# Four expert layers: router product turned round, low part of the router weights made later, sparse expert weights kept in fp32

## The reference

```python
x = x + _L0_ffn_ref(_layernorm(x), w12, w3, router_w, expert_bias, sw1, sw2, sw3)   # f1, f2
x = x + _L1_ffn_ref(_layernorm(x), gate_w, wg, wu, wd)                              # f3, f4

# f1, f2: a shared part of width 1024, and 8 routed experts of width 128, two for each token
shared_out = silu(x @ sw1.T) * (x @ sw2.T) @ sw3.T
scores = sigmoid(x @ router_w.T)                      # [1024, 8]
_, top_idx = top_k(scores + expert_bias, 2)
# f3, f4: 16 routed experts of width 128, two for each token, no shared part
scores = softmax(x @ gate_w.T)                        # [1024, 16]
topk_w, topk_idx = top_k(scores, 2)                   # then divided by their sum
# both: for each chosen expert e of token t, with weight c
y_t += c * (silu(x_t @ wg_e) * (x_t @ wu_e)) @ wd_e
```

## Time and profile before

| | us |
|---|---|
| median of three runs | 1898.88 (1898.35 to 1899.68) |
| the profiled execution | 1904.39 |
| its span | 1902.6 |
| PE busy in it | 1559.5 (82%) |
| DVE busy | 1293.0 (68%) |
| ACT busy | 931.7 (49%) |
| POOL busy | 680.3 (36%) |

### The profile page before, as it was taken

The page is one execution under the profiler, slowest core; times in us unless marked ns, Lnnn a source line. Parts: engine busy times, 40 slices in busy tenths (PEclk is TensorE's granted clock), DMA queues, the critical chain, the costliest instruction groups (busy, mean ns, idle before and its releaser), DMA issues. The chain is left out here.

```text
span 1902.6 us, 28081 instructions
## 1 busy us (share of the span) xinstructions
PE 1559.5 (82%) x9276; PEld 1211.8 (64%) x9286; DVE 1293.0 (68%) x2184; ACT 931.7 (49%) x2281; POOL 680.3 (36%) x711
## 2 busy tenths in 40 slices
PE   6899799879974665491679999999999999999472
PEld 5444478667851222480668888888888888887372
DVE  4665374666466998754647777777777777776652
ACT  2365345233524331451556666666666666665351
POOL 3011243315366773445823333222222233330173
PEclk9899799888986888595889999999999999999586
DMA  3220323223310000564000000000000000000463
GB/s 79 51 50 3 96 88 110 70 72 106 106 51 1 0 1 14 163 145 131 11 0 12 12 12 1 23 1 23 1 23 1 23 1 12 1 1 1 139 147 109
DMA packets 62057, 90.01 MB, mean 47 GB/s; under 512 B 10192, under 2 KB 44240, under 8 KB 61920
## 3 DMA queue, kind: packets, MB, share of 16 engines
q1 hardware_dynamic: 53664, 65.68, 11.6%
q0 software_dynamic: 8256, 22.56, 5.3%
HBM read 62.38 MB, written 19.40 MB: 43 GB/s over the span
## 5 line engine op out<-in xcount | busy, mean ns | idle before, releaser
L1295 DVE TENSOR_REDUCE gqa_neg_max<-acc 128x1 f32<-128x1024 f32 (+7 forms) x256 | 193.0, 754 | 173.8 <-PE acc L1404 172.7
L1181 ACT ACTIVATE gqa_probsT_high<-aux 128x512 fp32r<-128x512 f32 x288 | 172.0, 597 | 249.5 <-PE aux L1412 248.7
L1300 DVE TENSOR_TENSOR gqa_probsT_low<-aux,gqa_probsT_high 128x512 fp32r<-128x512 f32 x288 | 197.6, 686 | 29.8 <-ACT gqa_probsT_high L1181 25.6
L1190 ACT ACTIVATE gqa_probs<-acc,gqa_neg_max 128x1024 f32<-128x1024 f32 (+7 forms) x256 | 189.3, 740 | 29.7 <-DVE gqa_neg_max L1295 24.7
L1412 PE MATMUL aux<-ident,gqa_probs 128*128 128x128 f32 x1152 | 174.3, 274 | 0.0
L1088 POOL TENSOR_SCALAR gqa_q_scale<-gqa_q_scale 128x4 f32<-128x4 f32 x64 | 16.3, 255 | 382.1 <-ACT gqa_square L1125 381.8
L474 POOL DMA_INDIRECT f_xs<-tokens,f_slot_token x108 | 116.6, 1080 | 100.3 <-DVE f_slot_token L631 48.9
L1423 PE MATMUL aux<-gqa_probsT_high,gqa_v_high 128*128 128x512 f32 x288 | 146.5, 509 | 1.0 <-DVE gqa_probsT_low L1300 1.0
L1435 PE MATMUL aux<-gqa_wo,gqa_oT 128*128 128x256 f32 x512 | 133.3, 383 | 4.4 <-DVE stream L1288 3.5
L1092 POOL TENSOR_TENSOR gqa_ln_xn<-gqa_ln_xn 128x512 f32<-128x512 f32 x64 | 82.3, 1285 | 146.3 <-DVE gqa_ln_xn L1220 146.3
L1402 PE MATMUL acc<-gqa_k_low,gqa_q_high 128*128 128x512 f32 (+5 forms) x384 | 132.2, 344 | 0.0
(11 more groups left out here) (411 smaller groups left out, 4397.5 us busy)
## 6 DMA issues: line engine op xcount, KB each, us to landing
f_w<-in_f_up SPq DMA_DIRECT2D x64, 256.0 KB, 3.6
outputs_by_slot<-f_y_tile SPq DMA_DIRECT2D x108, 128.0 KB, 2.3
f_w<-in_f_down SPq DMA_DIRECT2D x64, 128.0 KB, 3.8
mat_qk<-mat_high SPq DMA_DIRECT2D x64, 64.0 KB, 2.3
tokens<-f_ln_xn SPq DMA_DIRECT2D x4, 1024.0 KB, 4.4
gqa_w_q<-in_g_wq SPq DMA_DIRECT2D x8, 512.0 KB, 3.5
gqa_wo<-in_g_wo SPq DMA_DIRECT2D x8, 512.0 KB, 3.8
mat_qk<-mat_low SPq DMA_DIRECT2D x32, 64.0 KB, 2.3
```

Source lines behind the costliest of these rows:

```text
L1181: act.activation(probsT_high[:, u % RING, :], aux[:, u % 2, :], ACT.Copy).then_inc(cell_high_ready, 1)
L1190: act.activation(out, scores(n), ACT.Exp, bias=neg_max[:, j % (2 * JOBS):j % (2 * JOBS) + 1], accum_out=row_sum[:, n // 2 % 4, m, n % 2:n ...
L1295: dve.tensor_reduce(neg_max[:, j % (2 * JOBS):j % (2 * JOBS) + 1], scores(n), AXY, ALU.max, negate=True).then_inc(max_ready, 1)
L1300: dve.tensor_tensor(probsT_low[:, u % RING, :], aux[:, u % 2, :], probsT_high[:, u % RING, :].bitcast(F32), ALU.subtract).then_inc(cell_lo ...
```

## The change

- The router's product is turned round. High and low parts of the router weights stand side by side in one tile, `w_router_parts`. They stand still, and 256 tokens run past them: `route_high` for the tokens' high part gives the products with both weight parts on 16 or 32 partitions, and `route_low` adds the tokens' low part times the high weights. They are issued between the transposes of the norm. ACT copies each result to `logits_by_expert` (which lies in `xs`, not yet in use), and `by_token` brings it back to a token on each partition, in fp32, with a matrix `sum_parts` that adds the two parts.
- The low part of the router weights and `sum_parts` are made within the norm on DVE, ahead of the first low part of the tokens.
- The routed experts' weights are loaded straight into `ws` in fp32. They are not split. One copy `part` in fp32 takes the place of `part_high` and `part_low`, and each product of three fp32r matmuls becomes one fp32 matmul. SP no longer waits for room in the ring for these experts. The ring and the splits stay for the shared experts.
- The copy to `y_tile` moves from ACT to DVE, behind `s_hidden`. In f3 and f4 Exp stands ahead of the splits' old place, with one Silu of one column behind it.

```diff
+            if q == 3 and before_low:
+                before_low()
             if q >= 3:
                 low(q - 3)
...
-            for m, e in enumerate(LOADS):
-                if m == STAGES:
+            for i, e in enumerate(LOADS):
+                if i == STAGES:
                     sp.wait_ge(norm.xn_ready, NT)
                     sp.dma_start(tokens_dram.rearrange("(n p) d -> p n d", p=P), norm.xn[:, :, :]).then_inc(xn_stored, 16)
+                if e not in place:
+                    sp.dma_start(ws[:, e - shared, 0:UP], up_dram[e:e + 1].rearrange("a p k n -> (a p) (k n)")).then_inc(ws_in, 16)
...
+                    continue
...
-                    act.activation(part_high[:, n % 3, cols], aux[:, n % 2, cols], ACT.Copy).then_inc(part_high_ready, 1)
+                    act.activation((part if PLAIN else part_high)[:, n % 3, cols], aux[:, n % 2, cols], ACT.Copy).then_inc(part_high_ready, 1)
...
-            dve.wait_ge(w_router_high_ready, 1)
-            dve.tensor_tensor(w_router_low[:, :, :], w_router[:, :, :], w_router_high[:, :, :].bitcast(F32),
-                              ALU.subtract).then_inc(w_router_low_ready, 1)
-            norm.vector(dve)
-            split(0)
...
+            norm.vector(dve, router_parts)
+            if shared:
+                split(0)
...
             else:
-                for m in range(1, E // 2):
-                    split(m)
                 dve.wait_ge(logits_ready, 1)
...
+                    if n >= 4 and PLAIN:
+                        m = n - 4
+                        dve.wait_ge(risen, n)
+                        if m >= 4:
+                            dve.wait_ge(y_stored[m % 4], 16 * (m // 4))
+                        dve.tensor_copy(y_tile[:, m % 4, :], aux[:, 2 + n % 2, D:2 * D]).then_inc(y_ready, 1)
...
-            for t in range(NT):
-                pe.wait_ge(norm.low_ready, t // 2 + 1)
...
-                    for m, (a, b) in enumerate(three(core.xnT_high[:, k, rows], core.xnT_low[:, k, rows],
-                                                     w_router_high[:, k, :], w_router_low[:, k, :])):
...
+            def route_high(q):
...
+                for k in range(DC):
+                    pe.matmul(route_banks[q][0:PAIR, 0:2 * P], w_router_parts[:, k, :],
+                              core.xnT_high[:, k, tokens], start=k == 0, stop=False, skip_group_check=True)
...
+            norm.tensor(pe, route)
+            route_low(2)
+            route_high(3)
+            by_token(0)
+            route_low(3)
+            for q in range(1, 4):
+                last = by_token(q)
             last.then_inc(logits_ready, 1)
```

More of the change, by code:

```diff
@@ L208, in tensor, with scalar @@
             last.then_inc(self.turned, 1)
-    def scalar(self, act):
+            if after:
+                after(q)
+    def scalar(self, act, after=None):
         c = self.core
@@ L232, in ffn_layer @@
     FRONT = 8
+    PAIR = 2 * routed
     LOADS = (0, 8, 9, 1, 10, 11, 2, 12, 13, 3, 14, 15, 4, 5, 6, 7) if shared else tuple(range(E))
-    place = {e: m for m, e in enumerate(LOADS)}
-    by_pool = [shared > 0 and e >= shared for e in LOADS]
+    PLAIN = True
+    RINGED = [e for e in LOADS if not (PLAIN and e >= shared)]
+    by_pool = [shared > 0 and e >= shared for e in RINGED]
+    place = {e: m for m, e in enumerate(RINGED)}
     splits = {2: (4, 5, 6), 3: (7, 8), 4: (9, 10), 5: (11,), 6: (12,), 7: (13,)}
@@ L246, in dense @@
         def dense(i):
-            steps.extend(("split", m) for m in splits.get(i, ()))
+            steps.extend(("split", place[LOADS[m]]) for m in splits.get(i, ()) if LOADS[m] in place)
             steps.extend([("up", i), ("silu", i)])
@@ L271, in sparse @@
             if shared and s in (2, 4):
-                steps.append(("split", 13 + s // 2))
+                steps.append(("split", place[LOADS[13 + s // 2]]))
             if s >= 1:
@@ L403, in w_split @@
         def w_split(m):
-            e = LOADS[m]
+            e = RINGED[m]
             if e >= shared:
@@ L460, in _ @@
                       allow_small_or_imprecise_dtypes=True).then_inc(numbers_made, 1)
-            for m in range(E):
+            for m in range(len(RINGED)):
                 if by_pool[m]:
@@ L510, in _ @@
             else:
-                for m in range(1, E):
-                    split(m)
+                act.wait_ge(shifted, 1)
+                act.activation(probs[:, :, :], select[:, :, :], ACT.Exp).then_inc(exp_ready, 1)
+                act.activation(s_silu[:, 0, 0:1], core.minus_half[:, 0:1], ACT.Silu)
             for kind, n in steps:
@@ L596, in _ @@
                 hide(0)
-                split(3)
+                split(place[1])
                 hide(1)
@@ L672, in _ @@
                                       ALU.subtract).then_inc(low_ready, 1)
-                elif kind == "part":
+                elif kind == "part" and not PLAIN:
                     cols = part_cols(n)
@@ L785, in rise @@
                         rows = slice(k * P, (k + 1) * P)
-                        for m, (a, b) in enumerate(three(part_high[:, r, rows], part_low[:, r, rows],
-                                                         *sparse_weights(s - 1, slice(k * 2 * P, (k + 1) * 2 * P)))):
-                            last = pe.matmul(aux[:, 2 + s % 2, 0:D], a, b, start=k + m == 0, stop=(k, m) == (DC - 1, 2))
+                        pairs = sparse_pairs(r, rows, s - 1, slice(k * 2 * P, (k + 1) * 2 * P))
+                        for m, (a, b) in enumerate(pairs):
+                            last = pe.matmul(aux[:, 2 + s % 2, 0:D], a, b, start=k + m == 0, stop=(k, m) == (DC - 1, len(pairs) - 1))
@@ L789, in rise @@
                 if s >= 4:
-                    for m, (a, b) in enumerate(three(part_high[:, r, D:], part_low[:, r, D:],
-                                                     *sparse_weights(s - 4, slice(UP, UP + D)))):
-                        last = pe.matmul(aux[:, 2 + s % 2, D:2 * D], a, b, start=m == 0, stop=m == 2)
+                    pairs = sparse_pairs(r, slice(D, D + P), s - 4, slice(UP, UP + D))
+                    for m, (a, b) in enumerate(pairs):
+                        last = pe.matmul(aux[:, 2 + s % 2, D:2 * D], a, b, start=m == 0, stop=m == len(pairs) - 1)
@@ new lines, in route_low, with by_token @@
+            def route_low(q):
+                tokens = slice(2 * q * P, (2 * q + 2) * P)
+                pe.wait_ge(norm.low_ready, q + 1)
+                for k in range(DC):
+                    last = pe.matmul(route_banks[q][0:routed, 0:2 * P], w_router_parts[:, k, 0:routed],
+                                     core.xnT_low[:, k, tokens], start=False, stop=k == DC - 1, skip_group_check=True)
+                last.then_inc(routed_ready, 1)
+            def by_token(q):
+                pe.wait_ge(parts_copied, q + 1)
+                for t in (2 * q, 2 * q + 1):
+                    last = pe.matmul(aux[:, 2, t * routed:(t + 1) * routed], logits_by_expert[:, t * P:(t + 1) * P],
+                                     sum_parts[:, :], start=True, stop=True, skip_group_check=True)
+                return last
```

111 lines of the change are left out of this document (71 added, 40 removed).

## The result

The changed kernel takes 1842.3 us (1839.2 to 1848.3, four runs) against 1899.3 for the kernel before; the ratio is 0.970, with a 95% interval of 0.968 to 0.972. It is 57 us faster where 90 were forecast, and it lies outside the range that was given (1790 to 1838). Run again beside the last experiments it took 1847.8, ratio 0.973 (0.971 to 0.975). The span of the profiled execution is 1837.4 us, 65 less than that of the profile before: it is the fastest of its four, and the one before was slower than its median.

What follows compares the result with a forecast made beforehand. The prediction took matmuls and the chain through ACT and DVE as the bound. Its terms, 11 + 22 + 9 + 21 + 14 + 13 = 90 us, took the profiled 1904.4 to 1814, or 1809 as median; range 1790 to 1838.

Steps and rivals of the forecast that it cites:

- The sparse tile: Sparse stages: fp32 products cut a tile from 1.575 to 1.08 us; 21 us in f1 and f2, 7.8 each in f3, f4.
- fp32 matmuls 0.22 apart: Sign in the changed kernel's profile that the forecast holds: fp32 matmuls on PE follow each other at 0.22 us.
- result copies stay 1.4 apart or more: Sign that the forecast is wrong: result copies of the sparse stages 1.4 us or more apart, against 1.08 and 1.25 forecast.
- Rival C: Sparse tiles: a plain fp32 product costs four passes, not two; 1.74 us a tile, kernel at 1862; chance 0.07.
- Rival B: Sparse tiles stay near 1.5 us because a wait takes the place of PE's work; kernel at 1846; chance 0.15.
- Norm's start: Front of each layer: with the router weights' low part made later, the norm starts with its layer; 11 us in all.
- Router: Front of each layer: a 4.7 us chain replaces 10.2 us of router matmuls; 5.5 us a layer, 22 in all.
- Middle of f1 and f2: f1 and f2: without POOL's splits, DVE and PE are not held up; 4.5 us a layer, 9 for two.
- The three effects that made up the 9: f1 and f2, per layer: 2.3 us of PE's wait, 0.8 of two shorter waits, 1.4 for the low-clock stretch.
- First gather of f3 and f4: f3 and f4: without DVE's eight splits behind the list, the first gather shortens to 0.95 us; 6.2 and 5.3 us.

Runs made afterwards that it cites:

- two_passes: The changed kernel, but f3 and f4 do each fp32 product as two fp32r passes over rounded weights, low parts left out (computed wrongly): 1832.8 us, 0.963 of before.
- front_only: The kernel before with the turned router and the low part of the router weights made within the norm; splits and three products kept: 1887.8 us, ratio 0.993.
- low_in_norm: The kernel before with one edit, DVE making the low part of the router weights within the norm: 1887.4 us, ratio 0.993.
- fp32_only: The changed kernel with the router and the start of the norm of the kernel before: 1880.9 us, ratio 0.989.

## Why the prediction was wrong, step by step

**The sparse tile: the step that failed.** The forecast priced a matmul at "(1.03 − 0.38)/3 = 0.217", with four matmuls behind the x4. They were two. The line is a loop over two heads in the code, and in the trace of the kernel before the group has 512 records for 256 matmuls:

```profile
L1435 PE MATMUL aux<-gqa_wo,gqa_oT x512: 378/379/764, 995.3 to 1767.7; 128*128 128x256 f32 x171
```

The right price from the same row is 0.433, and then 3 × 0.433 + 3 × 0.108 = 1.62 a tile, above the 1.575 it replaces. Term by term: 21 us forecast in f1 and f2 and 2 × 7.8 in f3 and f4; measured 1.5 us lost in all four. That is 38 us, more than the 33 by which the forecast missed; up to the first tile the layers gave 59.6 where 53.5 were forecast, 6 us back. Of the signs that the prediction named, "fp32 matmuls 0.22 apart" came true and meant nothing, since it counted records; "result copies stay 1.4 apart or more" (1.62) was the one that told. And with PE's work for a tile as small as forecast, f3 and f4 would not have given 7.8 each, but 4.5 and 7.0, by `two_passes`.

**Rival C was the mechanism.** It named four passes and gave 1.74 a tile and 1862. Its sign was right (PE bound, no gain from the tiles). Its time was 20 us too long: 14 in the sparse stages, mainly because it priced a product at 0.47, four times the 0.118 of fp32r, where 0.433 was measured (0.108 for each of four passes), and 6 because the front gave more. The rule of the Trainium skill ("FP8 and Floating Point Precision", "TensorE Precision Notes") that true FP32 takes four passes fits the trace well enough: 0.433 against 0.118 for one fp32r pass is 3.7. The prediction wrote that the trace does not agree with it; that was read from the row that had been miscounted. Rival B gave 1846, nearest of all, for a cause that did not occur: with less PE work the copies come 1.08 apart, so no wait had taken the place of PE's.

**Norm's start.** Forecast 11; the edit alone gave 14 (13.6 summed over the layers), and taken back from the changed kernel it cost 7 (10.4 summed over the layers). Right in size.

**Router.** Forecast 22. The logits come 9.6, 9.7, 8.0 and 9.4 us earlier; less what the norm's start gives by itself (3.7, 3.7, 1.9, 2.8) that is 24.6. Right in size, though only as this difference: no run turns the router alone. But the forecast added it to the rest as if it stood alone, and in f3 and f4 it is worth next to nothing unless DVE's splits go (up to the gather of the results `front_only` gives 3.4 and 3.4 us there, `low_in_norm` 3.2 and 3.0 without the turned router); the sum was right only because both edits were made.

**Middle of f1 and f2.** Forecast 9; the list comes 4.2 and 5.2 us earlier than the logits account for, and 4.0 and 3.8 in `fp32_only`. Right in size. The three effects that made up the 9 were not taken apart. The granted clock of f1's front is 0.89, against 0.78, which fits with a shorter stretch at the low clock.

**First gather of f3 and f4.** Forecast 6.2 and 5.3; from the list to the first tile f3 is 6.5 and f4 5.2 shorter. Right, and its cause is shown.

## What to carry to other kernels

Before a duration is divided by the count of a row, compare the count with the program: an fp32 matmul leaves two records, so one row of "x4" was two matmuls, and the price was off by a factor of two. Splitting into three fp32r products costs less on TensorE than one fp32 product (0.354 against 0.433 for 256 columns); what fp32 saves is the work around it, on other engines. And take a stage's edits together: removing one of two things that end at nearly the same time gives little, so that here 14.5 and 21.5 us apart made 57 together.

## What the runs showed of the hardware

A GpSimd gather stood still until 1 us behind a run of VectorE operations with two SBUF inputs (7.14 us beside a run of 7.02), and not beside one with an input in PSUM (1.13 beside 6.05). An fp32 product of 128x128 with 256 columns took 0.433 us and left two records, which is 0.108 for each of four passes; a product in fp32r took 0.118 and left one. Both are from sparse stages at the full clock. Where the difference per pass comes from was not tried.
